# Three queues for the transfers of a projection stage: value stores on ACT's, key stores on SP's, context loads on POOL's

## The chip, the cores and the metric
The kernel runs on one core of a Trainium2 chip. The metric is the device time of one execution in microseconds (us). The time before is the median of 3 runs. Every view shown comes from one profiled execution.

## What is computed
A gated cross-attention layer followed by a layer of experts, for 8 batch elements of 224 query rows and 750 context rows, 512 wide:

```python
x = x + jnp.tanh(g_xattn[0]) * _L0_xattn_ref(_layernorm(x), ctx_1024, ctx_1024, mask, W_q, W_k, W_v, W_o)
x = x + jnp.tanh(g_ffn[0]) * _L0_ffn_ref(_layernorm(x), gate_w, w_gate, w_up, w_down)
```

The part that matters here stands inside the attention: keys and values of the context, 16 heads of 32,

```python
K = proj(key, W_k)
V = proj(value, W_v)
emb_k = _rope_emb(K.shape[2], D_K)
K = _apply_rope(K, emb_k)
```

where `proj` is `einsum('bsd,ed->bse', x, W)` split into heads and `_apply_rope` is `x * cos + rotate_half(x) * sin`. What follows (scores, masked softmax, output projection, and 8 experts that each choose 56 rows per element) is not touched.

## The kernel before, in words
`program` runs three stages one after the other, each a block in which all engines start and end together: `project_context`, then `attend`, then `experts`. The change is inside `project_context`.

**Precision.** Matrix products are made from two parts each. A float32 tile x is copied to a high part (ACT) and x minus the high part becomes the low part (VectorE); TensorE then makes three products, high by high, high by low and low by high. So the context `c_raw` becomes `c_hi` and `c_lo`, the weights `w_hi` and `w_lo`, and the rotated keys are stored as the two parts of `k_split`.

**Loops.** The outer loop is over the 8 batch elements, in pairs: `i` is the pair (0 to 3), `j` the element in it, so the element is `2 i + j`. `pair` is written out for the first and the last pair and looped for the two between. Within an element there are 4 key groups (`g`, 128 key rows by 752 columns) and 6 value chunks (`c`, 125 context rows by 512). TensorE goes keys 0, values 0, keys 1, values 1, ..., keys 3, values 3, values 4, values 5 (L314 to L353).

**VectorE** rotates each key group (L277, L278, L280, L284: shuffle, times cosine, times sine, sum), makes the low part of the group before between those (L265), and after each group makes one chunk of the low part of the *next* element's context (`c_lo`, L259).

**ACT**, for each group: `copy_v` brings the value chunk from PSUM into `v_out` (L225), `high_k` makes the high part of the rotated keys (L218), `high_ctx` makes one chunk of the high part of the next element's context (L212). Chunks 4 and 5 of the values follow. The first `copy_v` of an element waits for all six value stores of the element before (`v_stored`), since there is one `v_out`:

```python
if c == 0:
    after(act, v_stored, 16 * KC * (2 * i + j))
```

The first matrix products of an element wait chunk by chunk for `c_lo` (L322).

**Transfers.** All but two are issued by SP, in a fixed order. At the start come `wk` and the first context in four chunks each, `wv`, the second context, and the two gains. Then for each element come the load of a context of the next pair, which waits until that buffer's low part is made (`ctx_lo`), and value store 0, key store 0, value store 1, key store 1, ..., value stores 4 and 5. `hold` makes the issue wait on a semaphore; each store waits for its own copy or low part. The query weights `wq` are issued by SP before the last pair. POOL issues the rotations and the constants (L189, L190). A key store moves 752 KB from 128 partitions, a value store 375 KB from 125 partitions, a context load 1500 KB. At the end SP waits for all key stores (`k_stored`) and all value stores.

Of the kernel before, what the change touches and what calls it, by code (L numbers as in the profile page):

```python
# [13 lines left out]
ds = bass.ds  # L14


B, S, D = 8, 224, 512
# [5 lines left out]
DC = D // P  # L23
QP, QC = 112, S // 112
KP, KC = 125, S2 // 125
KN = 376
SK = 2 * KN
HG, NG = 4, H // 4
# [28 lines left out]
def after(eng, sem, value):  # L57

    if not (isinstance(value, int) and value <= 0):
        eng.wait_ge(sem, value)  # L60
# [33 lines left out]
def project_context(nc, sem, sb, ps, ctxT, wk, wv, wq, wq_sb, wq_in, gx, gf, consts, rotations, kd, vd, cst, gains):  # L94

    with ExitStack() as st:
# [6 lines left out]
        c_raw = [sb(st, f"c_raw{j}", [P, DC, S2]) for j in range(2)]  # L103
# [5 lines left out]
        v_out = sb(st, "v_out", [KP, KC, 2 * VP, VB, DK])  # L109
# [7 lines left out]
        ctx_in = [sem(f"ctx_in{j}") for j in range(2)]  # L117
        ctx_hi, ctx_lo = sem("ctx_hi"), [sem(f"ctx_lo{j}") for j in range(2)]
# [4 lines left out]
        v_copied = sem("v_copied")  # L123
        k_stored = [sem(f"k_stored{j}") for j in range(2)]
        v_stored = sem("v_stored")

        def group(i, j, g):

            return 2 * NG * i + NG * j + g

        def turn(i, j, g):

            return NG * i + NG // 2 * j + g // 2

        def following(i, j):
            return (i, 1) if j == 0 else (i + 1, 0)

        with nc.Block() as block:
            @block.sync
            def _(sp):  # L140
                def hold(s_, v_):
                    sp.wait_ge(s_, v_)
                    sp.nop(nofuse=True)

                def load_ctx(i, j):
                    if not (isinstance(i, int) and i == 0):

                        hold(ctx_lo[j], DC * i)
                    sp.dma_start(c_raw[j][:], ctxT[ds(2 * i + j, 1)].rearrange("o p c n -> p (o c) n")).then_inc(ctx_in[j], 16)

                def store_k(i, j, g):

                    hold(klo_done[g % 2], turn(i, j, g) + 1)
                    sp.dma_start(kd[ds(2 * i + j, 1), g].rearrange("o h p n -> p (o h) n"), k_split[g % 2][:].bitcast(F32)).then_inc(k_stored[g % 2], 16)

                def store_v(i, j, c):
                    hold(v_copied, 2 * KC * i + KC * j + c + 1)
                    sp.dma_start(vd[ds(2 * i + j, 1)].rearrange("o a p (c n) -> p (o a) c n", c=KC)[:, :, c],
                                 v_out[:, c].rearrange("p (a q) e d -> p a (q e d)", a=2)).then_inc(v_stored, 16)

                def pair(i, last):
                    for j in range(2):
                        if not last:
                            load_ctx(i + 1, j)
                        for g in range(NG):
                            store_v(i, j, g)
                            store_k(i, j, g)
                        for c in range(NG, KC):
                            store_v(i, j, c)

                for c in range(DC):
                    sp.dma_start(wraw[:, 0, c], wk[:, c]).then_inc(wk_in[c], 16)
                    sp.dma_start(c_raw[0][:, c], ctxT[0, :, c]).then_inc(ctx0_in[c], 16)
                sp.dma_start(wraw[:, 1], wv).then_inc(wv_in, 16)
                load_ctx(0, 1)
                sp.dma_start(graw[:, 0:1], gx).then_inc(gains_in, 16)
                sp.dma_start(graw[:, 1:2], gf).then_inc(gains_in, 16)
                pair(0, False)
                with sp.Fori(1, B // 2 - 1) as i:
                    pair(i, False)  # L180
                sp.dma_start(wq_sb[:], wq).then_inc(wq_in, 16)
                pair(B // 2 - 1, True)
                for s in range(2):
                    sp.wait_ge(k_stored[s], 16 * B * NG // 2)
                sp.wait_ge(v_stored, 16 * KC * B)

            @block.gpsimd
            def _(pool):
                pool.dma_start(rot[:], rotations).then_inc(consts_in, 16)  # L189
                pool.dma_start(cst[:], consts).then_inc(consts_in, 16)  # L190
                for j in range(2):
                    nc.gpsimd.memset(c_hi[j][:, :, S2:SK].bitcast(F32), 0.0)
                    nc.gpsimd.memset(c_lo[j][:, :, S2:SK].bitcast(F32), 0.0)
                nc.gpsimd.memset(v_out[:, :, :, 1].rearrange("p c q d -> p (c q) d"), 1.0).then_inc(pads_set, 1)

            @block.scalar
            def _(act):
                def high_w(k, c):
                    if k == 0:
                        act.wait_ge(wk_in[c], 16)  # L200
                    elif c == 0:
                        act.wait_ge(wv_in, 16)
                    nc.scalar.activation(w_hi[:, k, c], wraw[:, k, c], ACT.Copy).then_inc(wsplit_hi, 1)

                def high_ctx(i, j, c):
                    if j == 0 and isinstance(i, int) and i == 0:
                        act.wait_ge(ctx0_in[c], 16)
                    elif c == 0:
                        act.wait_ge(ctx_in[j], 16 * (i + j))

                        after(act, v_made[j], KC * i)
                    nc.scalar.activation(c_hi[j][:, c, 0:S2], c_raw[j][:, c, :], ACT.Copy).then_inc(ctx_hi, 1)  # L212

                def high_k(i, j, g):

                    act.wait_ge(ksum_done, group(i, j, g) + 1)
                    after(act, k_stored[g % 2], 16 * turn(i, j, g))
                    nc.scalar.activation(k_split[g % 2][:, 0], k_cos[g % 2][:], ACT.Copy).then_inc(khi_done, 1)  # L218

                def copy_v(i, j, c):  # L220
                    act.wait_ge(v_made[j], KC * i + c + 1)
                    if c == 0:

                        after(act, v_stored, 16 * KC * (2 * i + j))
                    nc.scalar.activation(v_out[:, c, :, 0:VB:2, :],  # L225
                                         v_ps[(KC * j + c) % 4][0:KP, :].rearrange("p (q e d) -> p q e d", q=2 * VP, e=2),
                                         ACT.Copy).then_inc(v_copied, 1)

                def pair(i, last):
                    for j in range(2):  # L230
                        for g in range(NG):
                            copy_v(i, j, g)
                            high_k(i, j, g)
                            if not (last and j):
                                high_ctx(*following(i, j), g)
                        for c in range(NG, KC):
                            copy_v(i, j, c)

                for c in range(DC):
                    high_w(0, c)  # L240
                    high_ctx(0, 0, c)
                for c in range(DC):
                    high_w(1, c)
                act.wait_ge(gains_in, 32)
                nc.scalar.activation(gains[:], graw[:], ACT.Tanh).then_inc(gains_done, 1)
                pair(0, False)
                with act.Fori(1, B // 2 - 1) as i:
                    pair(i, False)
                pair(B // 2 - 1, True)

            @block.vector
            def _(dve):
# [1272 lines left out]
```

## Time and profile before

| What | us |
|---|---|
| Median of 3 runs | 2163.24 |
| Lowest and highest run | 2158.15, 2171.21 |
| The profiled execution's own time | 2161.29 |
| Its span (first to last instruction) | 2159.6 |
| TensorE busy | 1888.7 |
| VectorE busy | 1087.6 |
| ACT busy | 780.7 |
| POOL busy | 142.2 |
| Mean granted TensorE clock | 0.936 of full |

Names: PE is TensorE's matrix products, PEld its weight loads, DVE is VectorE, ACT is ScalarE, POOL is GpSimd, SPq is SyncE's queue. In a list of waits, "A <- B" says that A stood still until B was done. In an order of time, the bracket behind a row holds the idle time of the engine before it and what ended that. DMA share is the mean busy share of the core's 16 DMA engines. The clock is given as a share of full speed.

### The profile page before, as it was taken

To read this page: it belongs to the slowest core of one execution; us is meant where nothing else is said; L and a number is where in the kernel's file an instruction comes from. 1 tells how busy PE (TensorE), PEld (TensorE's weight loads), DVE (VectorE), ACT (ScalarE), POOL (GpSimd) and SP (SyncE) were. 2 spreads that over 40 slices of the span, in tenths; PEclk is the share of its full clock that TensorE was granted. 3 is DMA by queue.
4 is the path that set the end of the run, shared out by engine and by line. 5 is a ranking of instruction groups with operands and counts; after the bars stand their busy time and mean duration, and the time that the engine had idled before them with its cause. 6 is when DMAs were issued, how large, how long until landed. Compare 5 with 4: busy or idle time off the path is not lost. (4 is left out here: it accounts for less than half of the span.)

```text
span 2159.6 us, 29067 instructions
## 1 busy us (share of the span) xinstructions
PE 1888.7 (87%) x10136; PEld 1630.6 (76%) x10136; DVE 1087.6 (50%) x1901; ACT 780.7 (36%) x1246; POOL 142.2 (7%) x150
## 2 busy tenths in 40 slices
PE   7998973888887786888872999999999999999996
PEld 6887862766655565666651899999999999999995
DVE  5554542455655556665653444445353534444451
ACT  3221221444433443444430433434343434334341
POOL 0000000000000000000001002001020202020001
PEclk9999995899999998989895999999999999999998
DMA  6555447263444435363413334334343535343341
GB/s 234 179 181 190 155 163 172 82 162 108 126 110 116 123 92 138 92 170 92 113 31 102 108 115 124 116 108 140 107 141 107 141 107 141 107 129 110 111 125 22
DMA packets 86864, 269.34 MB, mean 125 GB/s; under 512 B 10968, under 2 KB 22968, under 8 KB 83488
## 3 DMA queue, kind: packets, MB, share of 16 engines
q1 hardware_dynamic: 77776, 244.77, 37.5%
q0 software_dynamic: 8992, 23.32, 4.8%
q8 instruction: 56, 0.92, 0.2%
q14 instruction: 40, 0.33, 0.0%
HBM read 199.29 MB, written 57.75 MB: 119 GB/s over the span
## 5 line engine op out<-in xcount | busy, mean ns | idle before, releaser
L1407 PE MATMUL gu_ps<-xs_hi,ws_hi 128*128 128x448 f32 x1024 | 372.1, 363 | 3.0 <-DVE xs_lo L1340 3.0
L1409 PE MATMUL gu_ps<-xs_hi,ws_lo 128*128 128x448 f32 x1024 | 372.0, 363 | 0.0
L1408 PE MATMUL gu_ps<-xs_lo,ws_hi 128*128 128x448 f32 x1024 | 371.4, 363 | 0.0
L786 DVE CUSTOM_DVE_ANT_0 junk<-m_ps,mq 112x752 f32<-112x752 f32 x256 | 232.0, 938 | 234.1 <-PE m_ps L1038 230.1
L1335 DVE TENSOR_TENSOR ws_lo<-w_raw,ws_hi 128x1024 fp32r<-128x1024 f32 x192 | 235.2, 1225 | 188.5 <-ACT ws_hi L1285 188.1
L659 ACT ACTIVATE e_t<-s_ps 125x448 f32<-125x448 f32 x384 | 202.6, 544 | 244.7 <-PE s_ps L1065 164.7
L1285 ACT ACTIVATE ws_hi<-w_raw 128x1024 fp32r<-128x1024 f32 x192 | 201.6, 1050 | 164.3 <-PE y_ps L1426 146.6
L1065 PE MATMUL s_ps<-qs,ks 128*125 128x224 f32 x768 | 221.3, 380 | 0.0
L1062 PE MATMUL s_ps<-mt,identb 125*125 125x448 bf16 x384 | 157.3, 410 | 67.0 <-ACT e_t L659 32.3
L1407 PEld LDWEIGHTS gu_ps<-xs_hi,ws_hi 128*128 128x128 f32 x1024 | 192.7, 188 | 15.8 <-issue 3.3
L1408 PEld LDWEIGHTS gu_ps<-xs_lo,ws_hi 128*128 128x128 f32 x1024 | 192.7, 188 | 13.4
L1409 PEld LDWEIGHTS gu_ps<-xs_hi,ws_lo 128*128 128x128 f32 x1024 | 192.8, 188 | 12.8
L1038 PE MATMUL m_ps<-ks,qs 96*112 96x376 f32 x512 | 136.8, 382 | 74.4 <-DMA ks<-k_split 37.9
L1424 PE MATMUL y_ps<-h_hi,ws_hi 128*128 128x448 f32 x512 | 186.0, 363 | 0.0
L1425 PE MATMUL y_ps<-h_lo,ws_hi 128*128 128x448 f32 x512 | 185.2, 362 | 0.0
L1426 PE MATMUL y_ps<-h_hi,ws_lo 128*128 128x448 f32 x512 | 185.2, 362 | 0.0
L1081 PE MATMUL o_ps<-e_t,vs 125*64 125x224 f32 x1536 | 179.7, 374 | 0.0
L1354 DVE TENSOR_TENSOR hid<-silu,gu_ps 128x448 f32<-128x448 f32 x128 | 79.5, 621 | 189.7 <-ACT silu L1306 189.7
L1306 ACT ACTIVATE silu<-gu_ps 128x448 f32<-128x448 f32 x128 | 69.8, 545 | 275.5 <-PE gu_ps L1409 275.5
L1065 PEld LDWEIGHTS s_ps<-qs,ks 128*125 128x125 f32 x768 | 160.6, 209 | 11.5 <-issue 2.0
L1038 PEld LDWEIGHTS m_ps<-ks,qs 96*112 96x112 f32 x512 | 88.5, 201 | 84.9 <-issue 51.0
L1062 PEld LDWEIGHTS s_ps<-mt,identb 125*125 125x125 bf16 x384 | 56.3, 147 | 112.9 <-ACT e_t L659 45.6
(132 smaller groups left out, 2570.4 us busy)
## 6 DMA issues: line engine op xcount, KB each, us to landing
w_raw<-wstream SPq DMA_DIRECT2D x192, 512.0 KB, 3.3
ks<-k_split SPq DMA_DIRECT2D x192, 188.0 KB, 3.9
k_split<-k_split SPq DMA_DIRECT2D x32, 752.0 KB, 3.6
v_pairs<-v_out SPq DMA_DIRECT2D x48, 375.0 KB
vs<-v_pairs SPq DMA_DIRECT2D x16, 1125.0 KB
c_raw<-ctxT SPq DMA_DIRECT2D x7, 1500.0 KB, 13.9
qs<-q_hi SPq DMA_DIRECT2D x64, 112.0 KB, 4.0
mq_raw<-maskq SPq DMA_DIRECT2D x8, 656.2 KB, 6.2
```

The source lines that it names most:

```text
L659: nc.scalar.activation(e_t[h % 4][:, pc], s_ps[n % 2][0:KP, 0:PAIR], ACT.Exp, scale=SCALE).then_inc(exp_at(b, h, pc)[0], 1)
L786: nc.vector.tensor_tensor_reduce(junk[u % 2][:].rearrange("p (a n) -> p a n", a=2), m_ps[u % 2][0:QP, :, 0:KN], mq[:, qc].rearrange("p (a ...
L1038: mm = nc.tensor.matmul(m_ps[u % 2][0:QP, n, 0:KN], qs[0:3 * WAYS, h, qc * QP:qc * QP + QP], ks[0:3 * WAYS, h % KSLOTS, n * KN:n * KN + KN ...
L1062: nc.tensor.matmul(o, identb[0:KP, 0:KP], mt[j][:, 2 * pc:2 * pc + 2, :].rearrange("p c s -> p (c s)"), start=True, stop=False)
L1065: mm = nc.tensor.matmul(o[:, k * S:k * S + S], ks[:, h % KSLOTS, c * KP:c * KP + KP], qs[:, h, :], start=False, stop=(k == 1))
L1285: nc.scalar.activation(w_hi[s][:], w_raw[s][:], ACT.Copy).then_inc(whi_done, 1)
L1335: nc.vector.tensor_tensor(w_lo[s][:], w_raw[s][:], w_hi[s][:], ALU.subtract).then_inc(wlo_done[s], 1)
L1407: nc.tensor.matmul(o, w_hi[s][:, w], xs_hi[:, c], start=(c == 0), stop=False)
L1408: nc.tensor.matmul(o, w_hi[s][:, w], xs_lo[:, c], start=False, stop=False)
L1409: mm = nc.tensor.matmul(o, w_lo[s][:, w], xs_hi[:, c], start=False, stop=(c == DC - 1))
L1424: nc.tensor.matmul(o, w_hi[s][:, w], h_hi[:, i], start=(i == 0), stop=False)
L1425: nc.tensor.matmul(o, w_hi[s][:, w], h_lo[:, i], start=False, stop=False)
```

## The change
The three kinds of transfer leave SP's single order. Key stores (and the loads of weights, gains and the first context) stay on SP. Value stores are issued by ACT: stores 0 to 3 behind `high_k` of the same group and ahead of `high_ctx`, stores 4 and 5 behind their copies. Context loads are issued by POOL: that of the second context between the rotations and the constants, the others in a loop that holds nothing but them. The wait for all value stores at the end moves from SP to ACT.

```diff
-                def load_ctx(i, j):
-                    if not (isinstance(i, int) and i == 0):
-
-                        hold(ctx_lo[j], DC * i)
-                    sp.dma_start(c_raw[j][:], ctxT[ds(2 * i + j, 1)].rearrange("o p c n -> p (o c) n")).then_inc(ctx_in[j], 16)
...
-                def store_v(i, j, c):
-                    hold(v_copied, 2 * KC * i + KC * j + c + 1)
-                    sp.dma_start(vd[ds(2 * i + j, 1)].rearrange("o a p (c n) -> p (o a) c n", c=KC)[:, :, c],
-                                 v_out[:, c].rearrange("p (a q) e d -> p a (q e d)", a=2)).then_inc(v_stored, 16)
-
                 def pair(i, last):
                     for j in range(2):
-                        if not last:
-                            load_ctx(i + 1, j)
                         for g in range(NG):
-                            store_v(i, j, g)
                             store_k(i, j, g)
-                        for c in range(NG, KC):
-                            store_v(i, j, c)
...
-                load_ctx(0, 1)
...
-                sp.wait_ge(v_stored, 16 * KC * B)
 
             @block.gpsimd
             def _(pool):
                 pool.dma_start(rot[:], rotations).then_inc(consts_in, 16)
+                pool.dma_start(c_raw[1][:], ctxT[1]).then_inc(ctx_in[1], 16)
                 pool.dma_start(cst[:], consts).then_inc(consts_in, 16)
...
+                def load_ctx(i, j):
+
+                    pool.wait_ge(ctx_lo[j], DC * i)
+                    pool.nop(nofuse=True)
+                    pool.dma_start(c_raw[j][:], ctxT[ds(2 * i + j, 1)].rearrange("o p c n -> p (o c) n")).then_inc(ctx_in[j], 16)
+
+                with pool.Fori(1, B // 2) as i:
+                    for j in range(2):
+                        load_ctx(i, j)
...
+                def store_v(i, j, c):
+                    act.wait_ge(v_copied, 2 * KC * i + KC * j + c + 1)
+                    act.dma_start(vd[ds(2 * i + j, 1)].rearrange("o a p (c n) -> p (o a) c n", c=KC)[:, :, c],
+                                 v_out[:, c].rearrange("p (a q) e d -> p a (q e d)", a=2)).then_inc(v_stored, 16)
+
                 def pair(i, last):
                     for j in range(2):
                         for g in range(NG):
                             copy_v(i, j, g)
                             high_k(i, j, g)
+                            store_v(i, j, g)
                             if not (last and j):
                                 high_ctx(*following(i, j), g)
                         for c in range(NG, KC):
                             copy_v(i, j, c)
+                            store_v(i, j, c)
...
                 pair(B // 2 - 1, True)
+                act.wait_ge(v_stored, 16 * KC * B)
```

How that stands on the engines, at the two places of which the prediction speaks. First, SP before, in the first pair, from the last group of element 0 into element 1 (`v_pairs` are value stores, `k_split` key stores, `c_raw` is a context load):

```order
L154 DMA k_split<-k_split 128x2x752 [waits klo_done0]
L158 DMA v_pairs<-v_out 125x2x384 [waits v_copied]
L154 DMA k_split<-k_split 128x2x752 [waits klo_done1]
L158 DMA v_pairs<-v_out 125x2x384 [waits v_copied] x2
L149 DMA c_raw<-ctxT 128x3000 [waits ctx_lo1]
L158 DMA v_pairs<-v_out 125x2x384 [waits v_copied]
```

The load stands behind the value stores of the element before. Now POOL's whole part of the stage with the change, from its first transfer to the branch that ends its loop:

```order
L171 DMA rot<-rotations 128x1504
L172 DMA c_raw<-ctxT 128x3000
L173 DMA cst<-consts 128x1028
...
L183 ISA [waits ctx_lo0]
L183 DMA c_raw<-ctxT 128x3000
L183 ISA [waits ctx_lo1]
L183 DMA c_raw<-ctxT 128x3000
L185 REGISTER_ALU
L185 COMPARE_AND_BRANCH
```

Every context but the first is loaded from here, each behind a wait for low context parts alone. Second, ACT before, at the last group of element 0 and the start of element 1:

```order
L225 ACTIVATE v_out<-v_ps 125x8x2x32 [waits v_made0]
L218 ACTIVATE k_split<-k_cos 128x752 [waits k_stored1,ksum_done]
L212 ACTIVATE c_hi<-c_raw 128x750
L225 ACTIVATE v_out<-v_ps 125x8x2x32 [waits v_made0] x2
L225 ACTIVATE v_out<-v_ps 125x8x2x32 [waits v_stored,v_made1]
```

and the same place with the change:

```order
L218 ACTIVATE v_out<-v_ps 125x8x2x32 [waits v_made0]
L211 ACTIVATE k_split<-k_cos 128x752 [waits k_stored1,ksum_done]
L224 DMA v_pairs<-v_out 125x2x384 [waits v_copied]
L205 ACTIVATE c_hi<-c_raw 128x750
L218 ACTIVATE v_out<-v_ps 125x8x2x32 [waits v_made0]
L224 DMA v_pairs<-v_out 125x2x384 [waits v_copied]
L218 ACTIVATE v_out<-v_ps 125x8x2x32 [waits v_made0]
L224 DMA v_pairs<-v_out 125x2x384 [waits v_copied]
L218 ACTIVATE v_out<-v_ps 125x8x2x32 [waits v_stored,v_made1]
```

A store now stands between the high part of the keys and that of the next context.

## Rows read from the trace of the kernel before

**Rows 1.** The page: busy time, share of the span, instructions.
```profile
PE 1888.7 (87%) x10136; PEld 1630.6 (76%) x10136; DVE 1087.6 (50%) x1901; ACT 780.7 (36%) x1246; POOL 142.2 (7%) x150
```

**Rows 2.** Order of time on POOL: start, duration in us, line, operation.
```profile
1.45 0.74 POOL L189 DMA_DIRECT2D rot<-rotations  x1 [0.86 <-POOLq L1518]
...
329.88 0.10 POOL L589 MEMSET minus_half<- 112x2 f32 x1 [325.56 <-POOLq L138]
```

**Rows 3.** Waits of ACT and of TensorE, 0 to 330 us: total, times, longest.
```profile
ACT v_out L225 <- DMA v_pairs<-v_out: 87.6, 6, 15.4
...
PE k_ps L322 <- DVE c_lo L259: 31.5, 10, 8.0
```

**Rows 4.** Order of time on ACT, element 4 and the starts of 5 and 7.
```profile
178.01 0.60 ACT L225 ACTIVATE v_out<-v_ps 125x512 f32<-125x512 f32 x1 [15.10 <-DMA v_pairs<-v_out]
178.51 0.82 ACT L218 ACTIVATE k_split<-k_cos 128x752 fp32r<-128x752 f32 x1
179.23 0.82 ACT L212 ACTIVATE c_hi<-c_raw 128x750 fp32r<-128x750 f32 x1
...
199.15 0.83 ACT L218 ACTIVATE k_split<-k_cos 128x752 fp32r<-128x752 f32 x1 [4.82 <-DVE k_cos L284]
...
217.12 0.60 ACT L225 ACTIVATE v_out<-v_ps 125x512 f32<-125x512 f32 x1 [15.45 <-DMA v_pairs<-v_out]
...
294.45 0.60 ACT L225 ACTIVATE v_out<-v_ps 125x512 f32<-125x512 f32 x1 [14.81 <-DMA v_pairs<-v_out]
```

**Rows 5.** Order of time on VectorE, element 4: low keys of group 2, last low context.
```profile
197.33 0.93 DVE L265 TENSOR_TENSOR k_split<-k_cos,k_split 128x752 fp32r<-128x752 f32 x1
...
200.73 0.94 DVE L259 TENSOR_TENSOR c_lo<-c_raw,c_hi 128x750 fp32r<-128x750 f32 x1 [1.61 <-ACT c_hi L212]
```

**Rows 6.** Order of time on SP's queue: start and duration of each issue.
```profile
52.18 2.78 SPq L149 DMA_DIRECT2D c_raw<-ctxT  x1
...
198.49 0.39 SPq L154 DMA_DIRECT2D k_split<-k_split  x1
199.19 0.26 SPq L158 DMA_DIRECT2D v_pairs<-v_out  x1
202.73 0.39 SPq L154 DMA_DIRECT2D k_split<-k_split  x1
203.43 2.18 SPq L158 DMA_DIRECT2D v_pairs<-v_out  x2
205.86 2.50 SPq L149 DMA_DIRECT2D c_raw<-ctxT  x1
...
245.55 2.16 SPq L181 DMA_DIRECT2D wq_sb<-wq  x1
```

**Rows 7.** Stretches: length, busy time per engine, clock, DMA share, GB/s.
```profile
184.50:185.50 1.00, 1.00 (x7) 1.00 (x6) 0.82 (x1) 0.14 (x1) 0.00 (x0) 1.00 0.00 0
...
187.50:190.00 2.50, 2.50 (x12) 2.03 (x11) 2.50 (x5) 0.00 (x0) 0.00 (x0) 1.00 0.32 73
190.00:192.30 2.30, 2.30 (x11) 1.81 (x10) 2.18 (x3) 0.00 (x1) 0.00 (x0) 1.00 0.29 99
...
199.40:201.40 2.00, 0.00 (x0) 0.00 (x0) 0.67 (x1) 2.00 (x4) 0.00 (x0) 1.00 1.01 384
201.40:204.20 2.80, 2.47 (x9) 2.48 (x10) 1.12 (x2) 0.27 (x1) 0.00 (x0) 0.67 0.31 71
...
209.70:213.30 3.60, 3.60 (x22) 3.55 (x21) 0.28 (x1) 0.00 (x0) 0.00 (x0) 1.00 0.95 370
```

**Rows 8.** Order of time on TensorE: first products of elements 0 and 5.
```profile
16.00 0.65 PE L322 MATMUL k_ps<-c_hi,w_hi 128*128 128x376 f32 x1 [0.36 <-DVE c_lo L259]
...
201.73 0.44 PE L322 MATMUL k_ps<-c_hi,w_hi 128*128 128x376 f32 x1 [4.62 <-DVE c_lo L259]
```

**Rows 9.** DMA issues, 200 to 217 us: number, size, us from issue to landing.
```profile
c_raw<-ctxT SPq DMA_DIRECT2D x1, 1500.0 KB, 14.8
```

**Rows 10.** The stretch of the first loads, columns as in rows 7.
```profile
2.00:16.00 14.00, 3.83 (x9) 2.47 (x10) 6.28 (x8) 5.78 (x9) 2.32 (x7) 1.00 0.99 368
```

## Prediction
> **What bounds the kernel now.** I read the page first: TensorE is busy 87% of the 2159.6 us span [rows 1], but that is a mean over three stages, and the change touches only the first, the projections. They end where POOL starts the next stage's work, at 329.88 us [rows 2]. So the views that count are those of the first 330 us.
>
> The waits of that stretch [rows 3] name the suspect: ACT stood 87.6 us in 6 waits of up to 15.4 us at its copy of values, released by the landing of value stores. TensorE's own idle time, 31.5 us at `k_ps` behind `c_lo`, is a consequence. To see how, read ACT's order of time [rows 4]. Call T the start of the first value copy of a batch element (element, below; they count from 0). It waits for all six value stores of the element before, so there are seven such T, of elements 1 to 7. From the T of element 4 at 178.01 us to that of element 7 at 294.45 there are three periods of 38.8 us.
>
> One period, from T = 178.01 to T' = 217.12, is one chain. (a) ACT and VectorE hand the four groups of an element to each other: high key part, `c_hi`, `c_lo`, the next rotation. The high key parts of groups 0 and 3 start at 178.51 and 199.15 [rows 4], 6.9 us a group. (b) The low key part of group 2 is done at 198.26 [rows 5], and SP issues key store 2 at 198.49 [rows 6], T+20.5. (c) From there the DMA engines work through key store 2, value store 3, key store 3 and value stores 4 and 5 [rows 6, 7] until T', 18.6 us later. TensorE begins the next element at 201.73, after a wait of 4.62 us [rows 8], and is not in this chain.
>
> The DMA shares deserve a slow look [rows 7]. While a key store runs the share is 1.01 at 384 GB/s. While only a value store runs, from 187.5 to 192.3 us, it is 0.32 and 0.29 at 73 and 99 GB/s. 0.31 is 5 of 16 engines: five engines carry every value store, 4.8 us each, and these five hardly rest. Whatever else they are given before T' moves T'. Now see where the context load stands. SP issues it at 205.86, behind value stores 4 and 5 in its own queue [rows 6], and it lands 14.8 us later [rows 9], at 220.7. From 209.7 to 213.3 the share is 0.95 [rows 7]: eleven engines do their part of the load beside the five that are still at value stores, and the five follow only after T'. 220.7 - 217.1 = 3.6 us is what the load costs the five, and today it falls behind T'.
>
> **The change part by part.**
> 1. *Context loads move to POOL.* POOL waits for the low context parts alone, done at 201.67 [rows 5], with nothing in front, so the load starts some 4 us earlier and beside value stores 3 to 5, not behind them. The five then have more than two value stores left, 9.6 us and up, so under any fair sharing the load's 3.6 us per engine are through before value store 5 lands. T' moves by 3.6 us. In how many periods? Six loads wait for an element's split. The one for element 2 waits for the very first split and meets only early stores. The other five (now issued from 52.18 to 205.86 us, first and last in [rows 6]) stand right before a T. 5 x 3.6 = 18.0 us. Bounds: 0 (the load hides in gaps of the five) and 4.2 each (1500 KB, all of it ahead, at 368 GB/s of [rows 10]), 21 in all.
> 2. *The query weights stay on SP*, but SP no longer stands behind value stores 4 and 5 of element 5 when it issues them (now 245.55 [rows 6]). 1024 KB against 1500 KB: 3.6 x 1024/1500 = 2.5 us before the T of element 6. Bounds 0 and 2.9.
> 3. *The load of the second context* is now behind `wk`, the first context and `wv` in SP's queue. POOL issues it between the rotations and the constants, at about 2.2 us by POOL's present pace (0.74 us from 1.45 [rows 2]). DMA is full from 2 to 16 us (share 0.99, 368 GB/s [rows 10]), and the first keys wait for the last chunk of the first context until 16.00 [rows 8]. 1500 KB put ahead of it are 4.2 us; I take 3.6, the load's own measure, since its end may not be wholly ahead. Bounds 0 and 4.2. The constants come later too, but VectorE asks for them only after the first keys, which shift as well. The gains no longer wait behind that load; the key chain doesn't hang on them, so that is worth nothing (cover: VectorE's first rotation).
> 4. *Value stores move to ACT.* Stores 0 to 3 are issued behind the high key part, not behind the key store of the group before. On SP store 3 was issued at 199.19, on ACT it comes after 199.15 [rows 4, 6]: the same within a us. Stores 4 and 5 go out some 2 us earlier (now at 203.43, in 2.18 us together [rows 6]). The five are busy then, so an earlier issue alone is worth nothing. What it may give: a value store runs at 73 GB/s in its first half and 99 in its second [rows 7], and with stores 3, 4 and 5 in one queue with nothing between, store 4 may skip the slow half. 187.5 KB at 99 instead of 73 GB/s save 0.7 us. I take 0.5 a period, 7 periods, -3.5 us, because the key store still shares the engines. Bounds: 0, and 2 stores x 0.7 x 7 = -10.
> 5. *The issue itself on ACT.* No row shows ACT issue a transfer. The nearest is SP's 0.26 us for value store 3 [rows 6]. On ACT it stands in the chain, between the high key part and `c_hi`. But the high part runs 0.82 us and `c_hi` starts 0.72 us behind it [rows 4]; the queue issues while it runs. I take 0. Below that nothing is possible, since nothing leaves ACT. If the cover is gone, four issues of 0.26 to 0.4 us (SP's for a key store, 0.39) in each of 7 periods are 7 to 11 us. SP and POOL have no work that an issue could hold up.
> 6. *After the last T* (294.45) no load is left, and the same six value and four key stores drain. 0.
>
> Sum: 18.0 + 2.5 + 3.6 - 3.5 = 20.6 us, say 21. The profiled execution took 2161.29 us (span 2159.6), 1.95 below the median of the three runs, 2163.24. Against the median: **2184 us**.
>
> A longer wait of TensorE at `c_lo` (4.6 to about 8 us) also costs clock: it stood at 0.67 from 201.4 to 204.2 and at 1.00 in the rows after 209.7 [rows 7]. The chain covers that, since T' comes 15.4 us after TensorE's restart.
>
> **A rule against this change.** Rows 7 show value stores and the context load on the same engines at one time. The Trainium skill (DMA: Bandwidth & Descriptors, section Issuing engines are not separate DMA queues) says that transfers issued from several engines run on the same 16 DMA engines and interleave, and that only sequencer time is saved. By that alone the change gives nothing, about 2163, which is the first rival. The same page (section Queues, rings and completion order) has a DMA engine go round its queues a packet at a time, which is term 1 in full. No row of this kernel shows how one engine divides its time between SP's, ACT's and POOL's queues.
>
> **The rivals.**
> - *No change.* The loads fit into time that the five engines have free, and T' stays. For it: from 184.5 to 185.5 us the DMA share is 0.00 [rows 7], so the five do rest about 1 us a period. Against: that rest lies before key store 2, not in the tail. Start-up may keep its 3.6. Time: 2162 to 2168.
> - *Faster: the tail packs better.* Value stores 3 to 5 stand in one queue, none gated by a key store, all at 99 GB/s (3.9 us, not 4.8), and loads fill only gaps. 3 x 0.9 x 7 = 19, less 3.6 at the start: 2148. It decides where the tail from key store 2 to T' falls under its 18.6 us. For it: the slow first halves. Against: the load must then cost nothing, though the five are busy to the end.
> - *Slower still: ACT pays for its issues.* Place and price of term 5; it decides where `c_hi` starts more than 0.72 us behind the high key part. 7 to 11 us on top: 2191 to 2195.
> - *The change doesn't do what it says.* POOL's load could start so late that it falls behind T' again. Against: POOL's first transfer took 0.74 us to issue [rows 2], far less than the 15 us between 201.7 and T'. Only start-up would be left, which the first rival holds.
>
> **How the numbers follow.** A measurement of this kernel can tell about 0.5%, 11 us, from no change. The forecast gets 0.58, ACT's stall on top of it 0.18, no change 0.14, better packing 0.10. The first two are slower by over 11 us: 0.76. The range reaches from no change, 2162, to the forecast's four upper terms, 18 + 2.5 + 4.2 + 11 = 35.7 without the gain of term 4: 2198. That leaves out most of the faster case and a little above.
>
> **What would show it.** Right: the period grows from 38.8 to about 42 us in front of the T of elements 2 to 5 and to 41 for element 6, and stays for element 7; ACT's wait for value stores goes from 87.6 to above 105 us; context loads land before T'; the first full keys start near 19.6, not 16.00. Wrong: a period that stays or shrinks, a load that lands after T', or a gap over 0.72 us between high key part and `c_hi` (then the issues count).

## The result and the profile after

The changed kernel takes 2188.03 us (median of 6 runs, 2178.19 to 2194.29) against 2163.89 us before: 1.011 times as long, 95% interval 1.0077 to 1.0143. That is 24 us more; the forecast was 21 more, 2184 us. The profiled execution is near the upper end of its runs, 2192.35 us with a span of 2190.8, so it is 31.1 us above the profiled execution of before, and its rows show a little more than the medians do. A median of the whole kernel and a row of one trace can differ by some us, so both are given where the argument hangs on it.

Where the time went: the next stage's first work on POOL.

```profile
358.16 0.10 POOL L590 MEMSET minus_half<- 112x2 f32 x1 [134.27 <-POOLq L138]
```

Against 329.88 before [rows 2] the projections end 28.3 us later. From there to the end of the span are 1832.6 us, against 1829.7. So 28.3 of 31.2 us are in the stage that was changed. The waits of 0 to 360 us, as in [rows 3], of ACT for value stores and of TensorE for the low context and the rotated keys:

```profile
ACT v_out L218 <- DMA v_pairs<-v_out: 122.8, 7, 18.9
...
PE k_ps L323 <- DVE c_lo L260: 37.9, 10, 8.1
PE k_ps L323 <- DVE k_cos L279: 11.8, 5, 4.8
```

ACT's wait for value stores grew from 87.6 to 122.8 us; the seventh such wait was put down to TensorE before and had 15.28 us, so 20 us are growth of the same seven. TensorE's wait at `c_lo` grew with them, from 31.5 to 37.9 us. Now ACT's order of time, the rows that answer to [rows 4]: the first value copies of elements 1, 5 and 7 and the last group of element 4.

```profile
71.12 0.60 ACT L218 ACTIVATE v_out<-v_ps 125x512 f32<-125x512 f32 x1 [16.96 <-DMA v_pairs<-v_out]
...
220.14 0.83 ACT L211 ACTIVATE k_split<-k_cos 128x752 fp32r<-128x752 f32 x1 [4.83 <-DVE k_cos L285]
220.35 0.27 ACTq L224 DMA_DIRECT2D v_pairs<-v_out  x1
220.88 0.81 ACT L205 ACTIVATE c_hi<-c_raw 128x750 fp32r<-128x750 f32 x1
221.59 0.58 ACT L218 ACTIVATE v_out<-v_ps 125x512 f32<-125x512 f32 x1
222.33 0.27 ACTq L224 DMA_DIRECT2D v_pairs<-v_out  x1
222.71 0.60 ACT L218 ACTIVATE v_out<-v_ps 125x512 f32<-125x512 f32 x1 [0.54 <-ACT v_out L218]
223.46 1.45 ACTq L224 DMA_DIRECT2D v_pairs<-v_out  x1
240.71 0.60 ACT L218 ACTIVATE v_out<-v_ps 125x512 f32<-125x512 f32 x1 [17.40 <-DMA v_pairs<-v_out]
...
322.08 0.60 ACT L218 ACTIVATE v_out<-v_ps 125x512 f32<-125x512 f32 x1 [17.24 <-DMA v_pairs<-v_out]
```

An issue on ACT takes 0.27 us, lies inside the key copy, and `c_hi` starts 0.74 us behind the start of that copy, as before (0.72). The issue of value store 5 takes 1.45 us; ACT has nothing to do behind it until T'. The seven starts T are at 71.12, 114.02, 157.26, 199.01, 240.71, 280.80 and 322.08 us: 8.5 us later for element 1, 27.6 for element 7. The mean period is (322.08 - 71.12) / 6 = 41.8 us. Before it was (294.45 - 62.59) / 6 = 38.6. The load in the tail of element 4, on POOL and in the list of DMA issues of 223 to 241 us:

```profile
223.36 0.53 POOL L183 DMA_DIRECT2D c_raw<-ctxT  x1 [41.21 <-DVE c_lo L260]
```

```profile
c_raw<-ctxT POOLq DMA_DIRECT2D x1, 1500.0 KB, 11.7
k_split<-k_split SPq DMA_DIRECT2D x1, 752.0 KB, 12.8
```

It lands at 235.1, 5.6 us ahead of T' = 240.71, where the load before landed 3.6 us behind T' [rows 9]. Key store 3 now lands 12.8 us after its issue (7.0 before). The stretches of that tail, columns as in [rows 7]:

```profile
220.80:222.40 1.60, 0.00 (x0) 0.00 (x0) 0.68 (x1) 1.37 (x3) 0.00 (x0) 0.82 0.98 372
223.00:225.00 2.00, 2.00 (x7) 2.00 (x8) 0.51 (x1) 0.30 (x1) 0.53 (x1) 0.50 0.30 58
227.00:230.00 3.00, 3.00 (x12) 2.52 (x11) 2.10 (x4) 0.00 (x0) 0.00 (x0) 0.73 1.04 377
230.00:233.00 3.00, 3.00 (x18) 2.82 (x17) 1.53 (x2) 0.00 (x0) 0.00 (x0) 1.00 0.78 287
233.00:239.20 6.20, 6.20 (x34) 5.64 (x33) 0.00 (x0) 0.00 (x0) 0.00 (x0) 1.00 0.32 124
239.20:240.70 1.50, 1.50 (x11) 1.50 (x10) 0.00 (x0) 0.00 (x0) 0.00 (x0) 1.00 0.12 46
```

The load runs with its full width at 227 to 230 us, then five engines alone work on at 0.32 for 6 us. The packets of 229 to 231 us (queue, kind: packets, MB, share of 16 engines) show the three queues side by side; q0 is POOL's with the load, q1 SP's with key store 3, q10 ACT's with value stores:

```profile
q0 software_dynamic: 45, 0.50, 74.3%
q1 hardware_dynamic: 51, 0.15, 19.0%
q10 hardware_dynamic: 16, 0.02, 4.7%
```

The load and the key store get nearly the same number of packets, and the value stores a third of it: they lie on 5 of the 16 engines, and 5/16 of 50 is 16. In front of T of element 7, where no load is left, the end of the tail looks otherwise:

```profile
318.50:321.50 3.00, 3.00 (x18) 2.77 (x17) 1.28 (x2) 0.00 (x0) 0.00 (x0) 1.00 0.07 25
```

A share of 0.07 is one engine of sixteen. For 3 us it works alone, and T waits for it. At the start, the last wait for the first context:

```profile
19.79 0.65 PE L323 MATMUL k_ps<-c_hi,w_hi 128*128 128x376 f32 x1 [0.35 <-DVE c_lo L260]
```

19.79 against 16.00 [rows 8].

### The profile page after: what moved, and what is told of

It is laid out like the page before. It is cut to its first block and busy times, and to the rows that moved or that the text cites. A ratio compares the mean times of both kernels' runs of the same rounds, so it can differ in the third digit from the quotient of the medians.

```text
span 2190.8 us, 29036 instructions
## 1 busy us (share of the span) xinstructions
PE 1890.0 (86%) x10136; PEld 1634.5 (75%) x10136; DVE 1087.9 (50%) x1901; ACT 781.5 (36%) x1246; POOL 144.6 (7%) x157
## 5 line engine op out<-in xcount | busy, mean ns | idle before, releaser
L1082 PE MATMUL o_ps<-e_t,vs 125*64 125x224 f32 x1536 | 173.3, 364 | 0.0
L323 PE MATMUL k_ps<-c_hi,w_hi 128*128 128x376 f32 x256 | 95.5, 373 | 49.7 <-DVE c_lo L260 37.9
```

## The experiments

Two theories stood at the outset of the experiments. **A**: a context load beside the value stores, on the five engines that carry them, moves the next value copy. **B**: key and value stores in two queues cost by themselves. B came from the period to element 7 in the changed kernel, 41.3 us against 38.4, in which no load is left; the prediction had that period unchanged. Times of an experiment are medians; ratios are to the kernel before, run on the same chip. T is always read from ACT's order of time.

### Hold the loads until the value stores have landed (loads_wait)

```diff
-                with pool.Fori(1, B // 2) as i:
+                for i in range(1, B // 2):
                     for j in range(2):
+                        if 2 * i + j > 2:
+                            pool.wait_ge(v_stored, 16 * KC * (2 * i + j - 2))
                         load_ctx(i, j)
```

> The changed kernel, but POOL also holds each context load until all value stores of the element whose tail it would meet have landed. Theory A (a load beside the value stores on the same five DMA engines moves the next value copy): the periods between first value copies of elements 2 to 5 fall back from 41.7 to 43.2 us to about 38.8, the start of the first value copy of element 1 from 71.1 to about 67, and the time from 2188 to about 2170 us (the late start of 4 us and something for the weights of the queries stay). Theory B (key and value stores in two queues are by themselves slower than in one): the periods stay above 41 us and the time within 5 us of 2188.

2180.47 us, ratio 1.0079 (1.0055 to 1.0102). T of element 1 fell to 67.66, as A says, but the periods to elements 2 to 5 only to 40.6 to 41.5, and the one to element 6, with the query weights, was 42.3:

```profile
67.66 0.60 ACT L220 ACTIVATE v_out<-v_ps 125x512 f32<-125x512 f32 x1 [13.84 <-DMA v_pairs<-v_out]
...
314.63 0.60 ACT L220 ACTIVATE v_out<-v_ps 125x512 f32<-125x512 f32 x1 [16.42 <-DMA v_pairs<-v_out]
```

A mean of 41.2 us. Taking the loads out of the tail gives some 8 us, and most of the loss stays: the time lies between the 2170 us of A and the 2188 of B. A alone is not enough.

### Move the loads alone (loads_only)

The kernel before, in which POOL has the context loads (the first waits for `wv_in`, so the start keeps its order) and SP keeps both kinds of store:

```diff
                     for j in range(2):
-                        if not last:
-                            load_ctx(i + 1, j)
                         for g in range(NG):
...
+                pool.wait_ge(wv_in, 16)
+                pool.dma_start(c_raw[1][:], ctxT[1]).then_inc(ctx_in[1], 16)
...
+                with pool.Fori(1, B // 2) as i:
+                    for j in range(2):
+                        load_ctx(i, j)
```

> The kernel before, with only the context loads moved to POOL (that of the second context held there until the value weights have landed, so that the start keeps its order); key and value stores stay in SP's one order. Theory A: the load again runs beside the last value stores, so periods of elements 2 to 5 are 42 to 43 us and the time is about 2164 + 5 x 3.6 to 4.5 = 2182 to 2186 us. Theory B: with one queue for the stores the periods stay at 38.2 to 39.1 us and the time at about 2164 us.

2182.43 us, ratio 1.0086 (1.0062 to 1.011), as A says:

```profile
66.73 0.60 ACT L228 ACTIVATE v_out<-v_ps 125x512 f32<-125x512 f32 x1 [16.05 <-DMA v_pairs<-v_out]
...
236.87 0.60 ACT L228 ACTIVATE v_out<-v_ps 125x512 f32<-125x512 f32 x1 [18.36 <-DMA v_pairs<-v_out]
...
315.16 0.60 ACT L228 ACTIVATE v_out<-v_ps 125x512 f32<-125x512 f32 x1 [13.91 <-DMA v_pairs<-v_out]
```

T of element 5 is 19.8 us later than before (217.12), for five loads: 3.9 us each. By the medians the whole is 18.5 us. The period to element 7, with no load in it, was below 38 (37.5). So A is real, with one queue for the stores, and B is absent there.

### The order of the start (start_order)

```diff
-                pool.dma_start(c_raw[1][:], ctxT[1]).then_inc(ctx_in[1], 16)
                 pool.dma_start(cst[:], consts).then_inc(consts_in, 16)
...
+                pool.wait_ge(wv_in, 16)
+                pool.dma_start(c_raw[1][:], ctxT[1]).then_inc(ctx_in[1], 16)
```

> The changed kernel with only the load of the second context held until the value weights have landed. The first full keys start near 16.0 us, not 19.8, every later time in the projections is about 4 us earlier than in the changed kernel, and the time is about 2184 us. If the start is hidden (the first value copy of element 1 waits for stores anyway), the copy of element 1 stays at 71.1 us and the time at 2188.

2183.81 us (1.0089, 1.0061 to 1.0117). The last wait of the first keys ended at 16.07, T of element 1 came at 65.52 (5.6 us earlier than in the changed kernel) and the stage ended at 353.02, 5.1 earlier. The median of the kernel is 4.2 us less. The start counts in full; nothing hides it. The periods kept their mean, 41.9 us against 41.8.

### Half a load (half_loads)

The looped loads bring only the first two of four chunks; the rest of each context is left out.

```diff
-                    pool.dma_start(c_raw[j][:], ctxT[ds(2 * i + j, 1)].rearrange("o p c n -> p (o c) n")).then_inc(ctx_in[j], 16)
+                    pool.dma_start(c_raw[j][:, 0:2], ctxT[ds(2 * i + j, 1)].rearrange("o p c n -> p (o c) n")[:, 0:2]).then_inc(ctx_in[j], 16)
```

> The changed kernel with the six looped context loads cut to the first two of four chunks (750 KB, not 1500; the other two chunks keep the data of an earlier element, so the output is not the reference's). A dose of half. Theory A: periods of elements 2 to 5 lie halfway between 38.8 and the 41.7 to 43.2 of the changed kernel, about 40.5, and the time falls by about 5 x 2 = 10 us to 2178. Theory B: periods and time as with whole loads.

2176.49 us (1.0052, 1.0017 to 1.0086). From element 2 to 5 the three periods have a mean of (233.80 - 114.30) / 3 = 39.8 us, against 42.2 in the changed kernel; the one before them did not shrink (42.9), nor did T of element 1 (71.45 against 71.12). In three of the five places a dose of half takes 2.4 us off, which speaks for A. But 39.8 is *below* the 41.1 that loads_wait, whose loads were held, has in the same periods. A and B don't add up, and the runs don't say by what rule they combine.

### Move the values alone (values_on_act)

The kernel before, value stores on ACT as in the change, everything else on SP:

```diff
                         if not last:
+                            if not (isinstance(i, int) and 2 * i + j == 0):
+                                hold(v_stored, 16 * KC * (2 * i + j))
                             load_ctx(i + 1, j)
                         for g in range(NG):
-                            store_v(i, j, g)
                             store_k(i, j, g)
```

> The kernel before, with only the value stores moved to ACT; key stores and context loads stay on SP, and each load is held until the value stores before it have landed, so that no load meets a tail. What the runs so far leave open is a second cost: with the loads held, the periods stayed at 40.6 to 41.5 us against 38.2 to 39.1 before. Theory B (key and value stores in two queues cost by themselves): periods 40.4 to 41.5 us for elements 2 to 7, time about 2164 + 7 x 2.3 = 2180 us. Rival (the rest came from POOL's issue of the loads): periods 38.2 to 39.1 and about 2164 us.

2176.52 us, ratio 1.0044 (1.0022 to 1.0066). Periods 39.4 to 42.5, mean (309.60 - 63.41) / 6 = 41.0 us. T of element 7 is 15.2 us later than before; by the medians the whole is 11.3 us. So B is real too, and POOL's way of issuing has nothing to do with it. The held loads are not its cause either: the period to element 7, which has no load, is the longest (42.5). The stretches before T = 309.60 show how it looks:

```profile
296.00:303.00 7.00, 7.00 (x38) 6.43 (x37) 3.71 (x6) 0.00 (x0) 0.00 (x0) 1.00 0.34 113
303.00:304.50 1.50, 1.50 (x8) 1.17 (x8) 1.50 (x3) 0.00 (x0) 0.00 (x0) 1.00 0.15 50
304.50:309.00 4.50, 4.50 (x27) 4.46 (x26) 0.37 (x1) 0.00 (x0) 0.00 (x0) 1.00 0.09 29
```

The end of the last of them by itself:

```profile
306.50:309.00 2.50, 2.50 (x16) 2.50 (x15) 0.00 (x0) 0.00 (x0) 0.00 (x0) 1.00 0.07 25
```

A share of 0.34 is the five engines, 0.15 some two of them, and 0.07 one (1/16 is 0.06). The five do not end together: two or one of them work on for 3.5 us, then one for 2.5 us while four rest, and the value copy waits for the last. How long the five are not all busy before T (a share under 0.26) differs from element to element, from 1 to 6.5 us here. Before the change only T of element 7 can be compared, since elsewhere the load or the query weights behind the stores fill the engines: it is 1.75 us there, with one engine alone for less than 1:

```profile
293.00:294.00 1.00, 1.00 (x7) 0.86 (x6) 0.81 (x1) 0.00 (x0) 0.00 (x0) 1.00 0.08 29
```

### Key store 3 last, in one queue (key_store_last)

```diff
-                        for g in range(NG):
+                        for g in range(NG - 1):
                             store_v(i, j, g)
                             store_k(i, j, g)
-                        for c in range(NG, KC):
+                        for c in range(NG - 1, KC):
                             store_v(i, j, c)
+                        store_k(i, j, NG - 1)
```

> The kernel before, all on SP, with key store 3 of each element moved behind value stores 4 and 5. Theory (whatever the five engines are given before the last value store moves the next value copy): key store 3, 2.0 us on each engine, falls behind it, so each of 7 periods is 2 us shorter, 36.2 to 37.1, and the time about 2164 - 14 = 2150 us. If the tail is set by the issue times or by the landing latency, nothing changes.

2148.49 us, ratio 0.9918 (0.9893 to 0.9942). Mean period (284.88 - 63.15) / 6 = 37.0 us, 1.7 less than before, for 2.0 us of key store taken out of the tail; five periods are 36.0 to 37.5 and one, to element 5, is 39.1, which stays unexplained. This is the same rule as A with the other sign, and a first gain.

### Key store 3 held, in two queues (key_store_held)

As values_on_act, and on SP:

```diff
-                        for g in range(NG):
+                        for g in range(NG - 1):
                             store_k(i, j, g)
+                        hold(v_stored, 16 * KC * (2 * i + j + 1))
+                        store_k(i, j, NG - 1)
```

> The kernel with only the value stores on ACT (run values_on_act), and SP holds key store 3 of each element until all six value stores have landed, so that its packets meet none of the tail. Theory B' (what two queues cost is the mixing of key and value packets on the five engines, after which one of them is last by several us): the mixing in the tail is gone and the periods are those of the run with key store 3 last in one queue, 36 to 37 us, time about 2150 us. Rival (a value store issued by ACT is slower whatever runs beside it): periods stay 2 to 2.5 us above those, 38.5 to 39.5, and about 2165 us.

2151.58 us, ratio 0.9941 (0.9914 to 0.9968). Mean period (278.50 - 59.78) / 6 = 36.5 us. With the mixing out of the tail, two queues are as good as one (37.0). From values_on_act it is 4.6 us a period less, where one queue gained 1.7 by the same move. So a value store issued by ACT is not slower by itself; what costs is key and value packets in two queues on the same five engines in the tail. Why one of the five then ends so late stays open: the trace has no engine number for a packet.

### Cut the value stores, in one queue (split_before)

```diff
-                    sp.dma_start(vd[ds(2 * i + j, 1)].rearrange("o a p (c n) -> p (o a) c n", c=KC)[:, :, c],
-                                 v_out[:, c].rearrange("p (a q) e d -> p a (q e d)", a=2)).then_inc(v_stored, 16)
+                    for r in (slice(0, 112), slice(112, KP)):
+                        sp.dma_start(vd[ds(2 * i + j, 1)].rearrange("o a p (c n) -> p (o a) c n", c=KC)[r, :, c],
+                                     v_out[r, c].rearrange("p (a q) e d -> p a (q e d)", a=2)).then_inc(v_stored, 16)
```

> The kernel before with each value store cut into two transfers, of 112 and of 13 rows, everything else in place. If the five busy engines are the cause, 112 rows go over all 16 engines (a share near 1.0 instead of 0.31 while a value store runs, some 1 to 1.5 us each), the tail shrinks from 18.6 to about 9 us, ACT's wait for value stores nearly goes, and TensorE sets the period at about 33.3 to 34 us: 7 x 4.8 to 5.5 us less, about 2126 to 2131 us. If a value store's time is set by its short rows and not by the number of engines, the share rises little and the time stays within 5 us of 2164.

2118.07 us, ratio 0.979 (0.977 to 0.981). The prediction's reading, that five engines carry every value store and set the period, is confirmed: the share while value stores run rises from 0.3 to most of the 16 engines (0.64 in the first row below, whose packets are all value rows and in which a store ends; 0.97 in the second, where three quarters are), the first value copy now waits for TensorE, and T comes every 33.2 us. The next stage starts at 287.23 us, 42.7 earlier than before. The time is 8 us below the 2126 to 2131 expected.

```profile
148.00:149.00 1.00, 1.00 (x6) 0.81 (x6) 0.51 (x1) 0.06 (x1) 0.00 (x0) 1.00 0.64 212
151.00:153.00 2.00, 2.00 (x13) 2.00 (x12) 0.00 (x0) 0.00 (x0) 0.00 (x0) 1.00 0.97 310
```

```profile
56.23 0.60 ACT L226 ACTIVATE v_out<-v_ps 125x512 f32<-125x512 f32 x1 [6.33 <-PE v_ps L336]
...
255.51 0.60 ACT L226 ACTIVATE v_out<-v_ps 125x512 f32<-125x512 f32 x1 [6.33 <-PE v_ps L336]
```

### Cut the value stores, in three queues (split_after)

The changed kernel with the same cut on ACT and the start as in start_order.

> The changed kernel (three queues) with the same cut of the value stores, and the load of the second context held as in the run on the start. If the five engines are what made the three queues dear, the loads no longer cost anything here: periods as in the run with one queue and cut stores, 33.3 to 34 us, and about 2126 to 2131 us. If three queues cost by themselves (Theory B in general), it stays 2 us a period above that one, some 2140 to 2145 us.

2145.16 us, ratio 0.9919 (0.9897 to 0.9942): 27 us above the same cut in one queue. That is the time that was expected of B (2140 to 2145), but not by B's 2 us in every period: it is the periods with a load that are long. T from element 5 to 7:

```profile
215.24 0.60 ACT L219 ACTIVATE v_out<-v_ps 125x512 f32<-125x512 f32 x1 [9.59 <-DMA v_pairs<-v_out]
...
251.97 0.60 ACT L219 ACTIVATE v_out<-v_ps 125x512 f32<-125x512 f32 x1 [8.42 <-DMA v_pairs<-v_out]
...
285.32 0.60 ACT L219 ACTIVATE v_out<-v_ps 125x512 f32<-125x512 f32 x1 [5.69 <-DMA v_pairs<-v_out]
```

37 to 38 us where a load meets the tail, 36.7 with the query weights, 33.35 with neither. All 16 engines carry the large part of a value store here, so five engines are not a condition for A. The packets of three queues in 210 to 212 us tell why, queues and columns as for the changed kernel:

```profile
q0 software_dynamic: 50, 0.60, 73.5%
q1 hardware_dynamic: 48, 0.14, 17.9%
q10 hardware_dynamic: 48, 0.07, 9.8%
```

50, 48 and 48 packets: that is what turns packet by packet give, whatever the size. A packet of the load has 12 KB (0.60 MB / 50), one of a value store 1.5 KB. So the load takes 74% of the engines' time and the value stores 10%. The Trainium skill (DMA: Bandwidth & Descriptors, section Queues, rings and completion order) has each DMA engine go round its queues a packet at a time. By these packet counts the trace agrees. The other cost here is on ACT, which issues two transfers in this place:

```profile
185.10 0.83 ACT L212 ACTIVATE k_split<-k_cos 128x752 fp32r<-128x752 f32 x1 [3.22 <-DVE k_cos L287]
185.31 1.50 ACTq L226 DMA_DIRECT2D v_pairs<-v_out  x2
186.85 0.83 ACT L206 ACTIVATE c_hi<-c_raw 128x750 fp32r<-128x750 f32 x1 [0.92 <-issue]
```

1.50 us do not fit under a copy of 0.83, and `c_hi` starts 1.75 us behind the start of the copy instead of 0.74.

### The same, with the loads held (split_after_wait)

> Three queues with cut value stores (run split_after), with each context load held until the value stores before it have landed. That run kept periods of 37 to 38 us where a load met the tail and 33.35 in the one period without. Theory A: without a load beside them the periods fall to 33.2 to 34 us and the time to about 2118 to 2122 us, that of one queue with cut stores. Rival (the double issues on ACT, which put the high part of the context 1.75 us behind the high key part instead of 0.72, are what costs): four such delays of 1 us stay in every period, 36 to 37 us, and about 2138 us.

The wait on `v_stored` of loads_wait, in split_after. 2129.73 us, ratio 0.9855 (0.9801 to 0.9908), between the same cut in one queue (2118.07) and split_after (2145.16). Five periods are 33.6 to 34.6 us and one, with the query weights that SP still issues into the tail, is 37.7. So the loads cost 3.4 to 4.4 us a period in split_after. The five periods have a mean of 34.0, 0.8 above the 33.2 of one queue: that is all that is left for the double issues, though no run shows them alone. A holds, and the rival has at most a small part.

### The cut in the next stage too (split_more)

One queue, cut stores, and the same two slices for the loads of value pairs and of the turned mask in `attend`, both of 125 rows, with their waits doubled to 32:

```diff
-                    sp.dma_start(vs[a][:].rearrange("p c q w -> p (c q w)"),
-                                 vd[ds(b, 1), a].rearrange("o p n -> p (o n)")).then_inc(vs_in[a], 16)
+                    for r in (slice(0, 112), slice(112, KP)):
+                        sp.dma_start(vs[a][r].rearrange("p c q w -> p (c q w)"),
+                                     vd[ds(b, 1), a].rearrange("o p n -> p (o n)")[r]).then_inc(vs_in[a], 16)
```

> The best kernel so far (one queue, value stores cut into 112 and 13 rows) with the same cut made in the next stage, for the two loads there that have 125 rows (value pairs, 1125 KB, 16 of them, and the turned mask, 656 KB, 8 of them). If these loads on five engines hold up the key loads queued behind them, the attention stage gets shorter by up to the 38 us that TensorE waits there for key loads; I expect 5 to 20 us, 2098 to 2113 us. If they are hidden, it stays at 2118.

2095.12 us, ratio 0.9678 (0.9627 to 0.9729): the best kernel of the study, 69 us below before, 93 below the changed one and 3 below the expected range. Its first stage ends as that of split_before, so what it adds lies in the next stage: 23 us by the medians (4 runs each, on two chips), 10 between the two profiled executions. TensorE's wait at its score maxima for key loads, in the waits of the whole span, first without and then with this cut:

```profile
PE m_ps L1039 <- DMA ks<-k_split: 30.6, 11, 9.0
```

```profile
PE m_ps L1041 <- DMA ks<-k_split: 16.0, 6, 3.0
```

That is 14.6 us less. Where the rest comes from, if the 23 of the medians hold, stays open.

## Why the prediction was right, and where it wasn't

- **The bound** was read rightly. One chain from T to T', its tail the DMA work of five engines. Two moves of key store 3 (37.0 and 36.5 us a period) and the cut of the value stores (33.2) each shifted T' the way that reading says.
- **Term 1, +18.0**, held. Moved alone, five loads made T of element 5 later by 19.8 us, 3.9 each where 3.6 was set. The mechanism, any fair sharing, was right, and the packet counts made it sharper: the sharing is by packets, so the load goes first. Beside value stores on ACT a load adds less: holding the loads made T of element 5 only 8.8 us earlier, 1.8 each.
- **Term 2, +2.5**, is not settled. The period to element 6 grew by only 1.2 us in the changed kernel (38.9 to 40.1), while the same weights cost some 3.7 us in split_after_wait. In loads_only, where they stay behind the value stores, it grew by 1.9 without them.
- **Term 3, +3.6**, held: 3.8 us at the first keys; the run without it is 4.2 us faster by the medians, and reaches its T and the end of the stage 5 to 6 us earlier.
- **Term 4, -3.5**, is the step that failed, in sign, though the total was met. Value stores 3 to 5 were to follow each other without the slow first half. The queue change costs instead: values alone on ACT made T of element 7 later by 15.2 us, 2.2 a period, as one of the five engines ends last. Its bounds, 0 to -10, did not hold a loss. With it failed one of the signs: the period to element 7 was to stay at 38.4 us and grew to 41.3. The others came true: 41.7 to 43.2 us for elements 2 to 5, 40.1 for element 6, a wait of 122.8 us for value stores, a load that lands before T', first keys at 19.79.
- **Term 5, 0**, held: an issue of 0.27 us under a copy of 0.83. The condition given with it, a gap over 0.72 us, was met here by 0.02 us, which costs nothing that can be seen, and in full in split_after, where there are two issues.
- **Term 6, 0**: 36.1 us from the last T to the next stage, against 35.4.
- **The sum** of 20.6 came near 24 since an unseen cost and an overlap met: loads alone put 23.0 us on the stage (352.85 at its end), values alone 15.5 (345.42), the start about 5, and all together 28.3, not 43. By the medians it is 18.5, 11.3 and 4.2, 34 in sum, against 24. The traces show part of the overlap: in front of T of elements 1 to 6 of the changed kernel, where a load or the query weights share the tail, one engine works alone for 0 to 1.75 us, in front of element 7, where nothing does, for 3 us. The loss of term 4 is smaller where that of term 1 or 2 is present; why is open. That the total was hit is partly luck. (The range's upper end comes to 2198.9 us by its own terms, not 2198.)
- **The rivals**: no change and better packing are out; ACT's stall did not occur. The first of them was drawn from the Trainium skill (DMA: Bandwidth & Descriptors, section Issuing engines are not separate DMA queues), by which transfers of several issuing engines interleave on the same DMA engines and only issue time is saved. That much agrees with the runs: nothing was gained on the path. It does not follow that nothing is lost: what lost was the order that one queue had kept.

## What to carry to other kernels

One queue is also an order: a transfer that nobody waits for soon, put in a queue of its own, no longer stands behind the one that is waited for, and if its rows are long it goes ahead of it. Before moving transfers, look at the DMA share while each runs alone; 0.31 is 5 of 16 engines, and cutting 125 rows into 112 and 13 in one stage was worth 47 us (2165.19 to 2118.07), where spreading over queues lost 24. Move what is not urgent behind what is, not beside it.

## What the hardware showed that was not expected

- Three queues on one set of engines were served packet by packet: 50, 48 and 48 packets in 2 us at 12, 3 and 1.5 KB each in split_after, 45, 51 and 16 in the changed kernel, whose value stores lie on 5 of 16 engines.
- With key and value stores in two queues the five engines no longer ended together: one engine alone, at a share of 0.07, for 2.5 us before T of element 7 in values_on_act and for 3 us in the changed kernel. With key store 3 out of the tail the loss was gone (36.5 us a period against 37.0 in one queue). Its cause is open.
- The costs of two such disturbances did not add: 23.0 and 15.5 us in the stage alone, 28.3 with a later start together.
- An issue on ACT takes 0.27 us, but the last of an element's six took 1.31 to 1.63 in the changed kernel (elements 1 to 6). Two issues in a row took 0.81 us in some places of split_after and 1.50 in the place under the key copy.
